# Mamba-2 block and ternary feed-forward: the first token block is turned and split later

## The reference

```python
zxbcdt = einsum('bld,ed->ble', u, W_in)            # z, x, B, C, dt
xBC = silu(conv4(xBC));  dt = softplus(dt + dt_bias)
y = ssd(x, dt, -exp(A_log), B, C, D)               # 8 heads of 128, state 64, chunks
yg = y * silu(z);  yn = yg * rsqrt(mean(yg*yg) + 1e-5) * norm_w
x1 = layernorm(u + einsum('ble,de->bld', yn, W_out))
wu, wg, wd = ternary_quant(W_up), ternary_quant(W_gate), ternary_quant(W_down)
out = layernorm(x1 + (silu(x1 @ wu.T) * (x1 @ wg.T)) @ wd.T)
```

## Time and profile before

| | us |
|---|---|
| median of 3 runs | 1446.06 (1445.99 to 1446.15) |
| the profiled execution | 1446.06 |
| its span, first to last instruction | 1444.3 |
| TensorE busy | 1363.7 (94%) |
| VectorE busy | 1142.9 (79%) |
| ScalarE busy | 798.7 (55%) |
| GpSimd busy | 636.8 (44%) |
| one tap of `conv` (L1718), mean of 192 | 0.749 |
| `add_squares` (L1553), mean of 56 | 1.274 |

### The profile page before, as it was taken

How to read it: one execution, slowest core, us unless ns; L and a number is a source line. 1 busy time by engine, 2 the same in 40 slices (tenths; PEclk the granted TensorE clock), 3 DMA queues, 4 the chain that set the end, 5 groups by cost and what they waited for, 6 DMA issues and landing times.

```text
span 1444.3 us, 27095 instructions
## 1 busy us (share of the span) xinstructions
PE 1363.7 (94%) x9514; PEld 878.3 (61%) x9514; DVE 1142.9 (79%) x1844; ACT 798.7 (55%) x1592; POOL 636.8 (44%) x628
## 2 busy tenths in 40 slices
PE   6897999999899999999999799999999999999997
PEld 3454555555555555556557577776767767676763
DVE  6986787887778868878785778888887978888884
ACT  5785474773756838658474454454544545454440
POOL 0574254573663737536265334343333424243231
PEclk9999999999999999999999999999999999999999
DMA  7456325262442633624344120101101010100001
GB/s 255 131 181 177 98 80 135 81 168 82 99 132 82 158 104 88 154 75 145 108 129 166 33 100 16 59 30 44 38 22 60 30 60 21 54 30 30 30 30 59
DMA packets 138007, 129.11 MB, mean 89 GB/s; under 512 B 40336, under 2 KB 110352, under 8 KB 136592
## 3 DMA queue, kind: packets, MB, share of 16 engines
q1 hardware_dynamic: 137872, 127.35, 30.0%
HBM read 99.93 MB, written 27.39 MB: 88 GB/s over the span
## 4 chain that ended last, share of the span: by engine, by line
PE 39%; DVE 23%; issue 18%; ACT 10%; POOL 4%; DMA 4%; SPq 1%; DVEq 0%; ACTq 0%; POOLq 0%
PE ring L1051 7%; PE ring L843 7%; PE ring L870 5%; PE p_turn L1035 4%; PE p_y L1035 4%; PE p_seg L1035 3%; PE p_st L1035 2%; DVE acc L1718 2%; ACT p_seg L1257 2%; ACT xdt L1248 2%; PE p_y L914 2%; DVE xdt L2057 2%; DVE xdt L2065 1%; PE p_y L922 1%; DVE seg L1816 1%
## 5 line engine op out<-in xcount | busy, mean ns | idle before, releaser
L843 PE MATMUL ring<-u_split,weights 128*128 128x512 f16 x1620 | 376.5, 383 | 0.4 <-DVE x_ch L1723 0.4
L843 PEld LDWEIGHTS ring<-u_split,weights 128*128 128x128 f16 x1620 | 155.8, 99 | 170.6 <-issue 8.4
L1636 POOL TENSOR_TENSOR xdt<-xdt 128x512 f32<-128x512 f32 x64 | 81.5, 1274 | 285.9 <-DVE xdt L2065 285.9
L1718 DVE SCALAR_TENSOR_TENSOR acc<-ring,taps,acc 128x511 f32<-128x511 f32 (+2 forms) x192 | 143.7, 749 | 4.5
L870 PE MATMUL ring<-w_out,raw 128*128 128x512 f16 x672 | 147.1, 379 | 0.0
L1248 ACT ACTIVATE xdt<-p_turn,dts 128x128 f32<-128x128 f32 x256 | 72.9, 375 | 84.0 <-PE p_turn L894 84.0
L870 PEld LDWEIGHTS ring<-w_out,raw 128*128 128x128 f16 x672 | 65.8, 99 | 77.6
L1545 POOL TENSOR_TENSOR raw<-yg,raw 128x512 f16<-128x512 f32 x64 | 78.8, 1231 | 74.4 <-ACT raw L1278 73.7
L1540 POOL TENSOR_TENSOR yg<-y_ch,z_ch 128x512 f32<-128x512 f32 x64 | 82.1, 1283 | 55.1 <-DVE y_ch L1838 55.1
L1442 ACT ACTIVATE grow<-xdt,tanh_scale 128x512 f32<-128x512 f32 x64 | 46.2, 722 | 91.4 <-DVE xdt L2057 91.4
L914 PE MATMUL p_y<-seg,xdt 128*128 128x128 f32 x512 | 69.6, 280 | 15.8 <-DVE seg L1816 15.6
(11 more groups left out here) (392 smaller groups left out, 3424.5 us busy)
## 6 DMA issues: line engine op xcount, KB each, us to landing
cum_rows<-cum_dram SPq DMA_DIRECT2D x64, 256.0 KB, 6.4
quant<-in_w_ffn SPq DMA_DIRECT2D x24, 512.0 KB, 4.5
quant<-in_w_ffn SPq DMA_DIRECT2D x48, 256.0 KB, 4.1
u_raw<-in_u_t SPq DMA_DIRECT2D x8, 1024.0 KB, 13.1
cum_g<-cum_dram SPq DMA_DIRECT2D x64, 128.0 KB, 7.2
rows<-in_u_tok SPq DMA_DIRECT2D x32, 256.0 KB, 4.8
x_dram<-rows SPq DMA_DIRECT2D x32, 256.0 KB, 2.0
tern_ug<-quant SPq DMA_DIRECT2D x32, 256.0 KB, 3.5
```

Source lines behind the costliest of these rows:

```text
L843: mm = pe.matmul(bank_k[:, :], w_in[:, ws, k, col:col + P], us[:, par, k * T:(k + 1) * T], start=(i == 0), stop=(i == 3 * KD - 1))
L1636: pool.tensor_tensor(tile_[:, 1, :, :], tile_[:, 0, :, :], tile_[:, 1, :, :], ALU.mult).then_inc(hid_ok, 1)
L1718: dve.scalar_tensor_tensor(acc[:, buf, k + 1:T], own[:, 0:T - 1 - k], taps[:, h, 2 - k:3 - k], acc[:, buf, k + 1:T], ALU.mult, ALU.add).th ...
```

## The change

Nothing is computed otherwise; the preparation of block 0 is put elsewhere.

- SyncE: the load of block 0 of x1 into u_raw moves from step 6, p = 3 to step 7, p = 0, behind the token loads; the wait for u_lo_ok in front of it goes.
- TensorE: the four turn_first leave p = 0 and p = 1 of step 7. One now stands behind each of the four chunk_out at the end of p = 1. USES_LAST follows.
- ScalarE: the four turned_first stand together behind signs of p = 1, followed by x_high 0 to 2 (before: 0 to 4). x_high(3) moves into p = 2 and x_high(4) into p = 3, both in front of conv_tanh of the odd head; x_high(5) stays behind signs of p = 3; x_high(6) moves into the tail, behind the last decays.
- VectorE: five x_low and four x_sum leave p = 1, where they stood among mean_square, residual and normalise. In p = 2 four operations stand behind the second within and three in front of quantise; in p = 3 two and one. x_low(6) moves behind the last within of the tail.
- The split with index 5 goes to acc and that with index 6 to b_tok; blocks with odd numbers shift their first two pieces within acc. The waits that guard these buffers follow.

```diff
-USES_LAST = ["x00", "x01", "t0", "t1", "x10", "x11", "t2", "t3", "ssq", "x20", "x21", "x30", "x31"]
+USES_LAST = ["x00", "x01", "x10", "x11", "ssq", "t0", "t1", "t2", "t3", "x20", "x21", "x30", "x31"]
...
-               ((xs_more[:, :], 0), (xs_more[:, :], 2), (c16, 0), (turn16, 0), (turn16, 2), (btok16, 0), (acc16, 4))],
+               ((xs_more[:, :], 0), (xs_more[:, :], 2), (c16, 0), (turn16, 0), (turn16, 2), (acc16, 0), (btok16, 0))],
...
-               ((acc16, 0), (acc16, 2), (thz16, 0), (thz16, 2), (c16, 2), (sq16, 0))]
+               ((acc16, 2), (acc16, 4), (thz16, 0), (thz16, 2), (c16, 2), (sq16, 0))]
...
+                        if is_at(n, NB - 1):
+                            sp.dma_start(u_raw[:, :].rearrange("p (c d) -> p c d", c=C),
+                                         x1_dram[0].rearrange("c p d -> p c d")).then_inc(xin_in, 16)
...
                         for c in range(1, C):
+                            if is_at(n, NB - 1):
+                                turn_first(c - 1)
                             chunk_out(n - 1, c)
+                    if p == 1 and is_at(n, NB - 1):
+                        turn_first(C - 1)
...
                     if j == 5:
+                        act.wait_ge(x_ok, NB * H - 1)
+                    if j == 6:
                         act.wait_ge(bdec_ok, NB * H)
-                    if j == 6:
-                        act.wait_ge(bc_ok, NB * 3)
...
-                    if is_at(n, NB - 1) and p < 2:
-                        turned_first(2 * p + 1)
+                    if is_at(n, NB - 1) and p >= 2:
+                        x_high(0, 0, p + 1)
...
-                    if is_at(n, NB - 1) and p in (1, 3):
-                        for j in range(5) if p == 1 else (5, 6):
+                    if is_at(n, NB - 1):
+                        for j in ((), (0, 1, 2), (), (5,))[p]:
+                            if j == 0:
+                                for k in range(KD):
+                                    turned_first(k)
                             x_high(0, 0, j)
...
             decays(NB, 0, 0, 1)
+            x_high(0, 0, 6)
...
+                    if is_at(n, NB - 1) and p >= 2:
+
+                        for j in ((0, 1), (4,))[p - 2]:
+                            x_low(0, 0, j)
+                            x_sum((0, 1, None, None, 3)[j])
...
+                    if is_at(n, NB - 1) and p >= 2:
+                        for j in ((2, 3), (5,))[p - 2]:
+                            x_low(0, 0, j)
+                        if p == 2:
+                            x_sum(2)
...
-            x_low(0, 0, 5)
             within(NB, 0, 0, 0)
-            x_low(0, 0, 6)
             for c in range(C - 1):
                 state_update(NB, 0, 0, c)
             within(NB, 0, 0, 1)
+            x_low(0, 0, 6)
```

More of the change, by code:

```diff
@@ L707, in step @@
                         load_utok(0, 1)
[L708 to L711, removed]
                     if p == 3 and more(n):
@@ L986, in step @@
                         states(n, p)
-                    if p < 2 and is_at(n, NB - 1):
-                        turn_first(2 * p)
                     if p == 2 and more(n):
@@ L996, in step @@
                         outputs(n, par, p)
-                    if p < 2 and is_at(n, NB - 1):
-                        turn_first(2 * p + 1)
                     if p == 2 and more(n):
@@ L1392, in step @@
                         gated(n, p, 0)
-                    if is_at(n, NB - 1) and p < 2:
-                        turned_first(2 * p)
                     if p == 1 and more(n):
```

## The result

| | before, us | after, us |
|---|---|---|
| median, same chip | 1446.11 (1445.99 to 1447.95, 4 runs) | 1460.51 (1455.03 to 1462.49, 4 runs) |
| the profiled execution | 1446.06 | 1461.22 |
| its span | 1444.3 | 1459.5 |
| granted clock, mean over the span | 0.991 | 0.985 |

The changed kernel is slower: ratio 1.0087, 95% interval 1.0066 to 1.0107. Forecast were 1459.2 us and a range of 1450 to 1463; all 4 runs lie in it. The record holds 31 executions of the changed kernel in all: median 1459.37, from 1453.80 to 1465.38, one of them above the range. (The ratio on record is nearer to that median than to 1460.51.)

A forecast was written before the change was run, and what follows sets the result against it. TensorE was taken to bound all four stretches around the last attention block. Latenesses of 1.7, 3.2, 1.3, 2.8, 1.8 and 2.4 summed to 13.2 (13.1 by clock times), so 1446.06 + 13.1 = 1459.2 us, range 1450 to 1463.

The forecast's parts named there:

- Parts 1 to 3: Transposes moved from p=0 and p=1 between the chunks, ScalarE's queue behind them: p=2's second seg 1.7 us late.
- Part 4: VectorE in p=2: four operations ahead of conv(7,5), lengthened by the port shared with GpSimd, delay turn_x(7,3,1) by 3.2 us more.
- Part 5: Three more VectorE operations before quantise(7,2) make the second seg of p=3 1.3 us later.
- Part 6: last_chunk(0,0): x_low(4) and x_sum(3) ahead of conv(7,7), waiting for x_high(4) and the port, add 2.8 us.
- Part 7: last_chunk(1,0): x_low(5), waiting 1.0 us for x_high(5), stands before the skips and adds 1.8 us.
- Part 8: First product: it waits for x_low(6), now at the end of VectorE's tail, adding 2.4 us.
- The load: x1 block 0 on SyncE's queue: lands near 683, 18 us before the first transpose; hidden.
- A row misread: Row at 753.85: an x_low takes 1.40 us instead of 0.60, lasting until GpSimd's multiplication is over.
- Rival A: In p=2 and p=3 the port costs nothing: +8.5, 1454.6 us; chance 20%.
- Rival B: Idle time of VectorE and ScalarE takes in all of parts 4 to 7: +4.1, 1450.2 us; chance 11%.
- Rival C: VectorE's queue made TensorE's waits in p=0 to p=2, and these go: 3.4 us faster, 1442.6; chance 3%.
- D: Feed-forward start, where VectorE is the bound (815 to 837): lateness partly caught up, within 0.2%; chance 6%.

The follow-up runs named there:

- Experiment 5: Changed kernel with the last of the four transposes in the middle of the last output chunk instead of behind it: 1461.48 us, ratio 1.0108.
- experiment 2: Changed kernel with GpSimd's y_low and add_squares of block 7, p=2 and p=3, cut to one column of 512: 1455.62 us, ratio 1.0081.
- experiment 1: Changed kernel with the old transposes, copies and load, only the splits at their new places: 1456.39 us, ratio 1.0097.
- experiment 3: Changed kernel with x_low(6) ahead of the state updates in VectorE's tail and x_high(6) behind x_high(5): 1455.91 us, ratio 1.0072.
- Experiment 4: Changed kernel with VectorE's x operations of p=2 and p=3 behind the odd head's silu, x_high(3) and x_high(4) behind signs of p=2: 1453.01 us, ratio 1.0054.
- experiment 6: Changed kernel with x operations behind the odd head's silu, last transpose inside the last chunk, seventh split ahead of the state updates: 1450.42 us, ratio 1.0033.
- experiment 7: Kernel before with VectorE's skips and state update of p=2 ahead of p=1's last residual in every block: 1441.87 us, ratio 0.9976.
- experiment 8: Changed kernel with the three moves of experiment 6 and the early skips of experiment 7: 1445.86 us, ratio 0.9998 against the kernel before.

## Why the prediction was right

Each part, as forecast, and as the table has it from mark to mark:

| part | forecast | measured |
|---|---|---|
| 1 to 3, to p=2's second seg | 1.7 | 1.61 |
| 4, to turn_x(7,3,1) | 3.2 | 2.88 |
| 5, to p=3's second seg | 1.3 | 1.29 |
| 6, first chunk | 2.8 | 2.72 |
| 7, second chunk | 1.8 | 1.74 |
| 8, first product | 2.4 | 2.58 |
| sum | 13.2, by the clock times 13.1 | 12.82 |

- **Parts 1 to 3: shown,** with a flaw in the weights. The transposes that left p=0 and p=1 gave 0.95 back for 1.05: sum_squares starts at 695.61 instead of 696.26, with its mark 0.30 later. Between the chunks each cost 0.44 for 0.49. From the last one to turn_x(7,2,0) it was 1.38 for 1.34 (718.44 to 719.82). The chain from x_dt to `seg` came out at 724.70, or 724.40 from the mark of the kernel before, for 724.5. Of this `seg`'s lateness of 1.83, though, 0.36 came with the last chunk's end, through the residual and the skips (720.99 before, 721.65 now), a path that the prediction did not add up; ScalarE's part was the other 1.47. Experiment 5 shows both: without ScalarE's wait `seg` follows the skips at once.
- **Part 4: shown.** The four operations took 4.44 us (731.50 to 735.94) for 4.8; the port's share was 4.44 - 2.59 = 1.85 for 2.2, with 2.59 from experiment 2 (728.60 to 731.19). Experiment 2 shows that the port made them long, experiment 1 that they delay turn_x(7,3,1) by 2.88 alone.
- **Part 5: right in size only.** It came out at 1.29 in the changed kernel and at 1.29 or 1.30 in experiments 1, 2 and 3, but no experiment takes its three operations out.
- **Parts 6 and 7: right in sum, less in their pieces.** The first chunk came at 759.58 for 759.75. Experiment 4 shows that part 6 hangs on where the operations stand: without them ahead of the conv it is gone (3.91 and 3.90 in the table). Part 7 lost only 0.6 by the same move, and its terms stay argued: x_low(5) waited 0.89 for x_high(5) where 1.0 was forecast. In place of part 6's wait of 1.0 for x_high(4) and 0.85 of port it was 1.77 and none: the two cover each other. In experiment 3 the same x_low waited 0.98 and then took 1.36.
- **Part 8: shown** by experiment 3, which takes it out whole: 2.58.
- **The load,** put at nothing, was hidden. It was issued at 674.81, as expected, but took 12.2 us instead of 7.8; it landed at 687.0, and the first transpose that needs it starts at 701.59.
- **A row misread without harm.** The x_low of 753.85 does not last until GpSimd's multiplication is over (753.43 + 1.27 = 754.70) but ends at 755.25, again 0.55 behind it. It waits for the other and then does its own work.
- **Rival A** (the port costs nothing) named +8.5 for a world without port waits; experiment 2 made that world, and it is 9.05 late. The rival's sum was sound, its premise false.
- **Rival B** (idle time absorbs parts 4 to 7) fell: 8.6 of the 12.82 us arose there. Experiments 4 and 6 show what it had of truth: placed behind the silu, the same work costs 3.5 us there.
- **Rival C** needed the waits of TensorE in p=2 to be made by VectorE's queue. They were, as experiment 7 shows, but by the skips, which the change leaves where they are.
- **D and the tail.** Nothing was caught up: 12.82 at the first product, and 1460.51 - 1446.11 = 14.4 between the medians. The prediction's sum has no term for the clock. The two traces show 1.24 of what lies beyond. Their next column sum, before and then in the changed kernel, is 14.06 us late from the marks:

```profile
778.04 0.95 PE L1061 MATMUL ring<-tri_ones,sq_sum 128*128 128x1 f32 x8
```

```profile
792.40 0.95 PE L1060 MATMUL ring<-tri_ones,sq_sum 128*128 128x1 f32 x8
```

  In experiments 1, 2 and 4, whose clock also drops behind the first product, the lateness grows by 1.23 over the same stretch. In 3, 6, 7 and 8, where it does not drop, it changes by 0.02 at most. The rest of the tail was not taken apart. That the whole time lies within 1.3 us of the forecast is in part luck: executions of one kernel spread by more, and the clock's part was not in the sum.

## What to carry to other kernels

The place of a piece of side work in an engine's queue can decide its price more than its length does. Here ten operations of 0.6 us cost 8.6 us with six of them ahead of what the bounding engine waits for, and 3.5 with all of them behind it. Most of the difference was the neighbour on the shared port. Before moving work into idle time, ask at which instruction of the row that idle time lies, and whether that neighbour is busy then. And where executions differ by more than the effect, compare traces from a mark just ahead of the edit.

## What the hardware showed unexpectedly

- **The clock fell behind TensorE's waits.** In the changed kernel TensorE idled 2.71, 2.56 and 2.51 us, and behind each the granted clock was 0.65 to 0.67 over 5 us. Full speed is 2.4 GHz, and within these stretches it stood at 0.50, the lower level of 1.2 GHz (772 to 774, for one): the projection of 12 matmuls at 742.78 took 4.44 us instead of 2.75. A stretch costs up to 5.0 x (1 - 0.66) = 1.7 us, and 1.24 were measured behind the first product. Over all the traces, a drop followed the wait of 2.5 us at the first product in each of the five kernels that had it, and none followed there in the other four experiments and the kernel before. Of the eight waits of 2.4 to 2.7 us before turn_x(7,3,1) and before the first chunk (changed kernel, and experiments 1, 3 and 5), four were followed by one and four not. So such a wait brings a drop often, not always; what decides was not found. In the changed kernel the first two drops were nearly hidden, as TensorE had to wait for VectorE next anyway: experiment 3 has the same two waits without a drop, and is 0.17 us sooner at both chunks.
- **Executions of the same code part by several us.** Experiment 3's trace came 2.3 us later to its mark than the kernel before, experiment 1's 5.1 sooner, with the same instructions up to there but for block 7's load. Nearly all of it had arisen by the first column sum, 141 us in. The 17 runs of the kernel before beside experiments 1, 2, 3 and 7 went from 1440.73 to 1449.28. A gain under 3 us needs many runs or a mark in the trace.
- **The port delays both sides.** GpSimd's add_squares took 1.71 us instead of 1.27 while VectorE ran x_sum. The prediction had priced VectorE's side alone.
